# A scatter of cache rows split by group, an index made first, and a weight load moved ahead of it

## What is computed

```python
# layer 0: attention over a paged cache, window 128, 8 query heads on 4 key/value heads of 32
q, k, v = x @ Wq.T, x @ Wk.T, x @ Wv.T          # rms norm and rotary position on q and k
pos = kv_lens[:, None] + arange(32)
blk = take_along_axis(block_tables, pos // 16, 1)
k_blocks = k_blocks.at[blk, :, pos % 16, :].set(k)   # the new rows go into the cache (v too)
k_all = k_blocks[block_tables]                       # then each sample reads its own blocks
scores = (q . k_all) * SCALE; masked to the last 128 positions; softmax; times v_all; @ Wo.T
x = x + that
x = x + weights1[cond].T-product over tokens         # layer 1: a 32x32 mixer chosen by sample
x = x + weights2[subj].T-product + bias              # layer 2: another
# layer 3: gated feed-forward with low-rank adapters chosen by sample
h = silu(x @ Wg + (x @ Ag[s]) @ Bg[s]) * (x @ Wu + (x @ Au[s]) @ Bu[s])
x = x + h @ Wd + (h @ Ad[s]) @ Bd[s]
```

## Time and profile before

| | |
|---|---|
| median of three runs | 253.76 us (253.05 to 255.38) |
| the profiled execution: its time | 252.41 us |
| the profiled execution: its span | 250.1 us (2.3 us lie around it) |
| mean granted TensorE clock | 0.965 |
| PE busy / DVE / ACT / POOL | 207.7 / 143.0 / 105.2 / 70.4 us |
| ad (L608): from issue to landing, median of eight | 3.6 us |
| DMA | 25.25 MB in 64124 packets, 55780 of them under 512 bytes |

### The profile page before, as it was taken

How to read it: one execution, slowest core, us unless ns; L and a number is a source line. 1 busy time by engine, 2 the same in 40 slices (tenths; PEclk the granted TensorE clock), 3 DMA queues, 4 the chain that set the end, 5 groups by cost and what they waited for, 6 DMA issues and landing times.

```text
span 250.1 us, 5105 instructions
## 1 busy us (share of the span) xinstructions
PE 207.7 (83%) x1995; PEld 187.9 (75%) x1995; DVE 143.0 (57%) x494; ACT 105.2 (42%) x291; POOL 70.4 (28%) x82
## 2 busy tenths in 40 slices
PE   2699978475865769959899799999979999899995
PEld 1577867364655658949789789888978988799994
DVE  5749878557656747285636644743664454326522
ACT  2163337656740573158323634632363463213310
POOL 3420047330038750176270443227040022000000
PEclk9999999859779999979999999999999999999999
DMA  6787899927983378899794012002200000010001
GB/s 167 219 173 110 187 190 239 320 73 160 136 222 93 105 182 120 195 202 190 130 156 111 3 42 66 0 3 73 76 1 3 0 3 0 3 42 3 0 3 42
DMA packets 64124, 25.25 MB, mean 101 GB/s; under 512 B 55780, under 2 KB 60836, under 8 KB 63524
## 3 DMA queue, kind: packets, MB, share of 16 engines
q1 hardware_dynamic: 60432, 14.07, 28.4%
q0 software_dynamic: 2944, 10.23, 16.1%
q10 hardware_dynamic: 724, 0.62, 0.8%
HBM read 17.83 MB, written 7.08 MB: 100 GB/s over the span
## 4 chain that ended last, share of the span: by engine, by line
PE 31%; issue 15%; DVE 13%; POOL 10%; DMA 5%; ACT 5%; SPq 4%; POOLq 1%
PE bank L1451 26%; POOL far L662 5%; SPq L542 4%; DMA early<-in_kb,blk_i 4%; POOL prob L676 3%; DVE prob L1084 3%; ACT prob L793 3%; DMA d_raw<-in_Wd 2%; DVE mask L1063 1%; PE bank L1437 1%; POOL near L665 1%; PE bank L1417 1%; POOL prob_near L677 1%; PE bank L1398 1%; DVE gs L1133 1%
## 5 line engine op out<-in xcount | busy, mean ns | idle before, releaser
L662 POOL DMA_INDIRECT far<-table_rows,place_i x32 | 31.5, 983 | 70.8 <-issue 37.2
L793 ACT ACTIVATE prob<-prob,ntop,qscale 128x160 f32<-128x160 f32 x64 | 32.4, 508 | 17.1 <-DVE ntop L1090 17.1
L1451 PE MATMUL bank<-xf_high,gu_high 128*128 128x256 f32 x128 | 39.1, 305 | 0.0
L1451 PE MATMUL bank<-xf_high,gu_low 128*128 128x256 f32 x128 | 36.3, 284 | 0.0
L1451 PE MATMUL bank<-xf_low,gu_high 128*128 128x256 f32 x128 | 36.3, 283 | 0.0
L1133 DVE SCALAR_TENSOR_TENSOR gs<-th,bank 128x256 f32<-128x256 f32 x32 | 13.4, 419 | 27.3 <-ACT th L828 27.0
L676 POOL TENSOR_TENSOR prob<-prob,rden 128x512 f32<-128x512 f32 x12 | 12.7, 1055 | 48.6 <-DVE rden L1109 48.6
L1451 PEld LDWEIGHTS bank<-xf_high,gu_high 128*128 128x128 f32 x128 | 24.6, 192 | 1.4 <-issue 1.0
L1451 PEld LDWEIGHTS bank<-xf_low,gu_high 128*128 128x128 f32 x128 | 24.5, 191 | 0.2
L1451 PEld LDWEIGHTS bank<-xf_high,gu_low 128*128 128x128 f32 x128 | 24.4, 191 | 0.0
L828 ACT ACTIVATE th<-bank 128x256 f32<-128x256 f32 x32 | 12.0, 380 | 24.3 <-PE bank L1451 24.3
(11 more groups left out here) (224 smaller groups left out, 523.2 us busy)
## 6 DMA issues: line engine op xcount, KB each, us to landing
table_rows<-early SPq DMA_DIRECT2D x32, 144.0 KB
table_rows<-far_probs SPq DMA_DIRECT2D x2, 512.0 KB, 3.6
gu_raw<-in_Wg SPq DMA_DIRECT2D x2, 512.0 KB, 5.2
gu_raw<-in_Wu SPq DMA_DIRECT2D x2, 512.0 KB, 5.7
d_raw<-in_Wd SPq DMA_DIRECT2D x2, 512.0 KB, 4.7
out<-xs SPq DMA_DIRECT2D x8, 128.0 KB, 1.9
xs<-in_x ACTq DMA_DIRECT2D x1, 512.0 KB, 5.0
xs<-in_x SPq DMA_DIRECT2D x1, 512.0 KB, 5.7
```

Of the source, the lines that this page charges most:

```text
L662: pool.indirect_dma_start(far[r][:, s, :], None, seen, bass.IndirectOffsetOnAxis(ap=far_i[:, GB * n + s:GB * n + s + 1], axis=0)).then_inc ...
L793: last = act.activation(v, v, ACT.Exp, bias=ntop[r][:, j:j + 1], scale=qscale[:, n, j:j + 1], accum_out=den[r][:, j:j + 1])
L1451: last = pe.matmul(dst, w[a], x[b], start=start and n == 0, stop=stop and n == 2)
```

## The change

1. The table holds one tile at a time: the 36 blocks of the tile's first group (4 samples x 9), then the 1024 new rows, then the 36 blocks of its second group. The area for odd tiles is gone.
2. A scatter is sixteen DMAs of 36 partitions: keys and values of the first group, then keys and values of the second. Each half has a semaphore of its own; the gather of a tile's first group waits for the first half alone. A load of blocks waits for both halves of the tile before.
3. SP waits before the scatter of tile t for the gathers of all groups of the tiles before it (for tile 3 that is a new count).
4. The bits that the block index does not need, the lengths as floats and what is made of them move behind the index on DVE; the index's matmul goes first on PE and alone; DVE waits for the rest by a second count of `slot_psum`.
5. `own_blk` leaves out the two last slots (72 columns where 88 were).
6. SP issues the down weights (d0, d1) ahead of tile 2's scatter.
7. In FIRST_ORDER ("den", 0) stands ahead of "up1" where it stood behind it.

```diff
-TILE_ROWS = BK * BLOCK
-TILE_AT = np.array([0, TILE_ROWS + B * T])
+HALF_ROWS = HB * BLOCK
+HALF_AT = np.array([0, HALF_ROWS + NEW_ROWS])
...
-     ("scores", 0), ("mask", 1), "gate1", ("first", 1), "up1", ("den", 0), ("prod", 1), "gate2", "up2",
+     ("scores", 0), ("mask", 1), "gate1", ("first", 1), ("den", 0), "up1", ("prod", 1), "gate2", "up2",
...
             def scatter_rows(t):
-                for raw, come, out_sem, at in ((k_raw, k_in, k_out, 0), (v_raw, v_in, v_out, KH)):
-                    sp.wait_ge(come, 16 * (t + 1))
-                    for g in range(G):
-                        lo = int(TILE_AT[t % 2])
-                        sp.dma_start(table_rows[lo:lo + TILE_ROWS, ...], raw[:, ...]).then_inc(out_sem[t], 16)
+                for half in range(2):
+                    lo = int(HALF_AT[half])
+                    own = slice(half * HB, (half + 1) * HB)
+                    for raw, come, at in ((k_raw, k_in, 0), (v_raw, v_in, KH)):
+                        sp.wait_ge(come, 16 * (t + 1))
+                        for g in range(G):
+                            sp.dma_start(table_rows[lo:lo + HALF_ROWS, ...], raw[own, ...]
+                            ).then_inc(rows_out[t][half], 16)
+
+            def next_rows(t):
+                for r in R:
+                    sp.wait_ge(kv_in[r], 16 * (GB + 1) * t)
+                scatter_rows(t)
...
-            scatter_rows(1)
+            next_rows(1)
             gate_up("g1", Wg, 0, upper)
             gate_up("u1", Wu, 1, upper)
-            def next_rows(t):
-                for r in R:
-                    sp.wait_ge(kv_in[r], 16 * (GB + 1) * 2)
-                scatter_rows(t)
-            next_rows(2)
             sp.wait_ge(mixer_psum, 2)
             for half in range(2):
                 sp.dma_start(d_raw[...], Wd[...]).then_inc(w_in[f"d{half}"], 16)
+            next_rows(2)
             sp.wait_ge(ssum_ready, SUMS)
...
             def load_blocks(t):
-                for dst, src, seen, done in ((k_raw, kb, k_out, k_in), (v_raw, vb, v_out, v_in)):
-                    if t:
-                        pool.wait_ge(seen[t - 1], 16 * G)
+                if t:
+                    for half in range(2):
+                        pool.wait_ge(rows_out[t - 1][half], 16 * 2 * G)
+                for dst, src, done in ((k_raw, kb, k_in), (v_raw, vb, v_in)):
...
-                pool.wait_ge(k_out[t], 16 * G)
-                pool.wait_ge(v_out[t], 16 * G)
+                for half in range(r + 1):
+                    pool.wait_ge(rows_out[t][half], 16 * 2 * G)
                 pool.wait_ge(new_out, 32)
...
-                seen = table_rows if t % 2 else table_rows[0:TILE_ROWS + NEW_ROWS, :]
+                seen = table_rows if r else table_rows[0:HALF_ROWS + NEW_ROWS, :]
...
             dve.wait_ge(lens_in, 16)
-            for k in range(12):
+            for k in range(11, 3, -1):
                 dve.tensor_scalar(bits[:, k:k + 1], ...)
-            then(len_i[:, 1:2] ...); then(len_f ...); four_len ...; diag_len ....then_inc(pos_ready, 1)
...
             then(dve.tensor_copy(blk[:, :], tab_f[:, 0:SLOTS]))
-            dve.tensor_tensor(own_blk ...)
-            dve.tensor_tensor(wblk ...).then_inc(slot_ready, 1)
+            dve.wait_ge(k32_in, 16)
+            dve.tensor_tensor(own_blk ...).then_inc(slot_ready, 1)
+            dve.tensor_tensor(wblk ...)
+            dve.tensor_scalar(len_i[:, 1:2] ...); four bits
             dve.wait_ge(slot_psum, 1)
             dve.tensor_copy(blk_i[:, :], small("slots", BP)).then_inc(blk_ready, 1)
+            then(len_f ...); four_len ...; diag_len ....then_inc(pos_ready, 1)
+            dve.wait_ge(slot_psum, 2)
             then(dve.tensor_copy(wblk_f[:, :], small("writer", NW)[:, 0:1]))
...
             pe.wait_ge(ones_set, 1)
+            pe.wait_ge(slot_ready, 1)
+            pe.matmul(small("slots", BP), own_blk ...).then_inc(slot_psum, 1)
             pe.wait_ge(pos_ready, 1)
+            pe.matmul(small("writer", NW)[:, 0:2], wblk ...)
             pe.matmul(small("writer", NW)[:, 2:4], ..., len_f[:, 0:2])
             pe.matmul(small("pos"), ..., four_len)
             pe.matmul(small("lens"), ..., diag_len)
-            pe.wait_ge(slot_ready, 1)
-            pe.matmul(small("slots", BP), own_blk ...)
-            pe.matmul(small("writer", NW)[:, 0:2], wblk ...)
             pe.matmul(wblk_rows, ones[0:B, 0:NW], wblk ...).then_inc(slot_psum, 1)
```

More of the change, by code:

```diff
@@ L34 @@
 BK = BT * OLD
-BP = BT * SLOTS
+HB = GB * OLD
+BP = 2 * HB
 BACK = WINDOW // BLOCK
@@ L165 @@
 MIX_BANKS = ((1, 1), (0, 2))
-SMALL = {"slots": (0, 0, NT), "writer": (0, 4, 8), "later": (0, 8, 24), "pos": (7, 0, NG), "lens": (7, 32, 64), "subj": (6, 64, 96),
+SMALL = {"slots": (0, 0, NT), "writer": (6, 4, 8), "later": (0, 8, 24), "pos": (7, 0, NG), "lens": (7, 32, 64), "subj": (6, 64, 96),
          "scale": (6, 96, 224), "rows": (0, 224, 224 + WIDTH), "place": (0, 400, 400 + B + NG), "bias": (0, 440, 448),
@@ L395, in build @@
         v_in = sem("v_in")
-        k_out = [sem(f"k_out{t}") for t in range(NT)]
-        v_out = [sem(f"v_out{t}") for t in range(NT)]
+        rows_out = [[sem(f"rows_out{t}_{half}") for half in range(2)] for t in range(NT)]
         new_out = sem("new_out")
@@ L550, in new_rows @@
                 sp.wait_ge(k_ready, half + 1)
-                lo = TILE_ROWS + half * NEW_ROWS // 2
+                lo = HALF_ROWS + half * NEW_ROWS // 2
                 sp.dma_start(table_rows[lo:lo + NEW_ROWS // 2, :].rearrange("(g p) c -> p g c", p=P),
@@ L634, in load_blocks @@
             def load_blocks(t):
-                for dst, src, seen, done in ((k_raw, kb, k_out, k_in), (v_raw, vb, v_out, v_in)):
-                    if t:
-                        pool.wait_ge(seen[t - 1], 16 * G)
+                if t:
+                    for half in range(2):
+                        pool.wait_ge(rows_out[t - 1][half], 16 * 2 * G)
+                for dst, src, done in ((k_raw, kb, k_in), (v_raw, vb, v_in)):
                     pool.indirect_dma_start(dst, None, src.rearrange("n g o d -> n (g o d)"),
-                                            bass.IndirectOffsetOnAxis(ap=blk_i[0:BK, t:t + 1], axis=0)).then_inc(done, 16)
+                                            bass.IndirectOffsetOnAxis(ap=blk_i[:, t:t + 1], axis=0)).then_inc(done, 16)
             pool.wait_ge(blk_ready, 1)
@@ L997, in _ @@
             won, own = small("rows", B), c3("own")
-            then(dve.scalar_tensor_tensor(moved_by[:, :], won, float(TILE_ROWS - 1), own, ALU.add, ALU.subtract))
+            then(dve.scalar_tensor_tensor(moved_by[:, :], won, float(HALF_ROWS - 1), own, ALU.add, ALU.subtract))
             then(dve.scalar_tensor_tensor(moved_by[:, :], won, 0.0, moved_by[:, :], ALU.is_gt, ALU.mult))
@@ L1210, in _ @@
             pe.wait_ge(ones_set, 1)
+            pe.wait_ge(slot_ready, 1)
+            pe.matmul(small("slots", BP), own_blk[:, :, :, :].rearrange("s h j b -> s (h j b)"), c3("tile"), start=True,
+                      stop=True).then_inc(slot_psum, 1)
             pe.wait_ge(pos_ready, 1)
+            pe.matmul(small("writer", NW)[:, 0:2], wblk[:, :, :].rearrange("s w n -> s (w n)"), ones[0:B, 0:2],
+                      start=True, stop=True)
             pe.matmul(small("writer", NW)[:, 2:4], c3("spread_writer"), len_f[:, 0:2], start=True, stop=True)
@@ L1214, in _ @@
             pe.matmul(small("lens"), ones[0:B, :], diag_len[:, :], start=True, stop=True)
-            pe.wait_ge(slot_ready, 1)
-            pe.matmul(small("slots", BP), own_blk[:, :, :].rearrange("s j b -> s (j b)"), c3("tile"), start=True, stop=True)
-            pe.matmul(small("writer", NW)[:, 0:2], wblk[:, :, :].rearrange("s w n -> s (w n)"), ones[0:B, 0:2],
-                      start=True, stop=True)
             pe.matmul(wblk_rows, ones[0:B, 0:NW], wblk[:, :, :].rearrange("s w n -> s (w n)"), start=True, stop=True
```

34 lines of the change are left out of this document (18 added, 16 removed).

## The result

The changed kernel took 261.06 us (median of four, 260.76 to 261.22) where the kernel before took 254.57 us beside it (253.05 to 258.66): ratio 1.027, interval 1.021 to 1.034. The forecast was 249.0 us, in a range of 245.5 to 253.0. Six more executions of the same kernel, beside others, gave 260.48 us and 1.030 (1.025 to 1.034). The loss is some 7 us.

The account below looks back on a forecast made before the run. TensorE was taken as busy for 83% of the span, with named waits as the winnable part. Gains 0.7 (net of the start's loss), 1.9 and 3.2 less 1.0 make 4.8 us: 253.76 to 249.0 us, range 245.5 to 253.0.

Parts of the forecast that it names:

- The start: Block index up to the first gather: later small matmul groups delay DVE and the first transposes, loss 0.8 us.
- Split, on tile 1: Group 2's gather starts at 70.1 instead of 72.52 us; TensorE's idle time shrinks, gain 0.7 us net of the start.
- `den` first: Group 2's softmax: GpSimd scales earlier, TensorE's idle 1.32 and 0.88 us go, gain 1.9 us.
- Down weights first: Before group 3's scores: ScalarE's 3.24 us wait and TensorE's idle 2.87 us go, gain 3.2 us.
- `ad` late: Additive weights behind tile 2's scatter on SP land at 112.9 us, wanted at 111.6: loss 1.0 us.
- Tile 3's scatter: Its new wait for group 5's gather stays covered before group 6's gather, by 2.9 us: effect 0.
- a half costs SP as much as a whole: Rival on the scatter's issues on SP: time near 262 us at 1.08 us each, near 256 at 0.95; chance 0.12.
- 88.9 + 32p: That rival's landing time of the additive weights in us, p being SP's us per scatter issue; gain gone at 0.89.

Follow-up runs that it names:

- the fast orders: GpSimd's gather of group 4 and load of tile 3 behind den(1): 0.980 in the kernel before with down weights and den first, 0.988 in the changed kernel.

## Why the prediction was wrong

The milestones say which steps held. The second execution of the changed kernel started within 0.5 us of the one before, so it is the one to compare (us from the span's start):

| | before | after | after, again |
|---|---|---|---|
| queries' projection | 25.59 | 28.89 | 26.08 |
| group 2's gather starts | 72.52 | 72.76 | 69.92 |
| group 2's keys on TensorE | 80.54 | 84.67 | 81.26 |
| output mixing of pair 0 | 100.50 | 104.19 | 99.45 |
| exps of group 3 | 113.31 | 113.80 | 109.07 |
| scaling of group 3 | 115.86 | 116.34 | 114.55 |
| split of `ad` | 117.37 | 125.17 | 123.81 |
| span | 250.1 | 258.8 | 258.4 |

**The start** (loss 0.8): right. `blk_i` came at 6.12, forecast 6.2, the product with `later_same` at 10.77, forecast 10.7, and in the second execution the first gather at 34.44, 0.85 us later than before. The further 2.5 us in the profile of after are its clock, not the change: TensorE leaves its lower level (1.2 GHz) some 6 us later there (the eight of L1253 took 3.69 us where the same took 1.99 before), and other programs with an equal start differ in the same way, see the end.

**Split, on tile 1** (gain 0.7 net): wrong by 1.4 us. Group 2's gather started at 69.92, forecast 70.1, but its keys reached TensorE 0.7 us later than before, not 0.7 earlier. The gather now lies beside the second half of the scatter: its five issues took from 69.92 to 77.31 where they took 72.52 to 78.67, and the last landed 4.8 us after its issue, where before TensorE went on 3.0 us after it.

**`den` first** (gain 1.9): from group 2's keys to the output mixing 19.96 us before, 18.19 again: 1.8 won. Right.

**Down weights first** (gain 3.2): from the mixing to the exps 12.81 before, 9.62 again and 9.61 after: 3.2 won. Right, and in the second execution TensorE's granted clock is 1.00 from 92 to 110 us.

**`ad` late** (loss 1.0): this is the step that failed. It was forecast to land at 112.9 and landed at 123.8 in the second execution: 10.9 us too late. Three terms of it: SP got to the scatter at 92.18 instead of 90.1 (2.1), since the mixers' product, for which it waits ahead of `d`, ended at 90.4 and not at 88.5; the scatter took 15.1 us instead of 10.7 (4.4), as an issue costs 0.76 us at least, not 0.67, and some are held; and the eight issues and the last landing took 16.5 instead of 12.05 (4.4), which is tile 3's load beside them. With the load moved the third term is gone (9.4 us, from 105.83 to 115.2): `ad` is then 2.3 us later than forecast, and the kernel is faster than before (0.992). So the dear issues alone don't make the loss. What made it is that I took `ad`'s 8.45 and 3.6 us over from the kernel before, and put tile 3's load beside them at nothing. I had read the 0.67 from rows of 512 runs; the runs above say that 576 aren't on a line with them. A half took 0.76 us at the median, 0.89 as a mean over tile 2's sixteen (14.28 us) and 0.945 in the second execution (15.12 us). The 0.95 for 64 KB that I had set beside it, from the Trainium skill, "DMA: Bandwidth & Descriptors", section Bandwidth, is the time that the DMA engines are busy with one load that GpSimd issues; as an estimate for SP's issue of a half it is near the second of these means and above the median.

**Tile 3's load ahead of the scaling:** not in my sum at all. I had followed GpSimd for groups 2 and 3 and stopped there. Yet the load is released by the scatter that I was making later, and the scaling stands behind it in one queue. In the changed kernel the held scaling (2.94 us on TensorE) is covered by the wait for `ad`; it is what other orders ran into. Each run that made tile 2's scatter later without touching this order gained nothing (1.003, 1.008, 1.016).

**Tile 3's scatter** (0): right in the changed kernel; group 6's gather was released by TensorE, not by the scatter.

The rival "a half costs SP as much as a whole" had the sign, the place and nearly the price: `ad` at 88.9 + 32p, and 0.89 as the point from which it decides. At the 0.81 us a scatter's sixteen really took on tile 1 it gives 114.8, which would still have been a gain; it needed the landing beside the load as well. I had given it 12%. Its formula isn't my sum with another price, either: at 0.67 it gives 110.3 where the sum has 112.9, because it leaves out SP's wait for the mixers (90.1) and GpSimd's own queue.

What stays open: why one issue takes 0.63 us for 32 partitions and 0.76 for 36; why TensorE's lower clock falls into 95 to 100 us in some profiles and not in others; and how much of the gain in the fast orders is `den`'s.

## What to carry to other kernels

When a change makes a transfer land later, list every instruction on every engine that waits for it, and then what is queued behind each: the price is paid by the work behind the waiting instruction and by the transfers beside the one that it starts, here a 1 us scaling and eight small weight loads, for a tile that SP took up only 18 us after it had landed. An early prefetch isn't free in an in-order queue. And a part that gains nothing alone (0.998) or loses (1.037) may be worth 2% in company, so test orders in pairs.

## What was not expected of the hardware

- Issues on SP aren't priced by size: medians of 0.63 us for 512 runs, 0.76 for 576, a least of 0.78 for 1152 (median 1.08); and single ones take 2 to 4 us while GpSimd's indirect transfers run (`ad` in the two profiles of the changed kernel: 582 to 3719 and 583 to 4060 ns), one of them 7.5 us in the kernel with the split alone.
- TensorE's clock at the start rose about 6 us apart in executions of programs with an equal start (the changed kernel itself: projection at 28.89 and 26.08). The projection started at 25.0 to 25.6 us in four profiles that keep the order of the start, and at 27.9 and 28.0 in two; with the index part at 26.1 to 26.7 in eight and at 28.7 to 28.9 in three. With TensorE kept busy it was 24.5 to 25.1 in three of three, too few to call it settled. The column of the granted clock says 1.00 for all of 0 to 20 us in every one of them, so there only the products' durations tell it.
